# Tabled places for the side streams of an attention turn, and 22 idle products a turn, in a transformer block with routed experts

## The chip, the cores and the metric

The kernel runs on one core of one Trainium2 chip. The metric is the device time of one execution in microseconds. The core has five engines with one instruction row each, which wait for one another by semaphores: TensorE (PE; its weight loads are PEld), VectorE (DVE), ScalarE (ACT), GpSimd (POOL) and SyncE (SP), which here only issues DMAs.

## What is computed

Sixteen sequences of 512 tokens with 128 channels pass through one block: a modulated layer norm, causal attention with 16 heads of 8 channels and rotary positions, a gated residual; then a second norm and a feed-forward layer in which every token goes to 8 of 160 experts, beside one shared expert.

```python
mod = (silu(c) @ wmod)                         # sa, ca, ga, sb, cb, gb for each sequence
h = layernorm(x) * (1 + ca) + sa
q, k, v = split(h @ qkv_w.T + qkv_b)           # q and k rotated (apply_rope)
attn = softmax(where(causal, q @ k.T / sqrt(8), -1e9))
x = x + ga * ((attn @ v) @ proj_w.T + proj_b)
h = layernorm(x) * (1 + cb) + sb
top_w, top_idx = top_k(sigmoid(h @ router_w.T + bias), 8)
x = x + gb * (sum over the 8 experts of silu(h @ w_gate) * weight @ w_down + shared(h))
```

## The kernel before, in words

The program has two parts. The first goes through the attention and the routing of all sequences, in turns numbered -2 to 16; the second runs the experts over pages of 128 gathered tokens and adds up their results. The change touches only the first.

**The core of a turn.** Turn i does two things side by side. It finds the row maxima of the scores of sequence i+1, in 40 units of one bank each: TensorE multiplies q by k (L558, bf16, into banks 0 and 1, called MX), and VectorE takes the maximum (the custom instruction at L568, which writes rmax). And it computes the exponentials of sequence i (the first ten units still of sequence i-1), again 40 units: TensorE multiplies k by q with the maxima folded in (L645, into banks 2 to 4, called ST), adds the causal mask by small products (L657), and ScalarE takes the exponential (L672, which writes prob). The units go in pairs. A pair of maximum products comes first, then a pair of score products, 20 of each in a turn; I count them from 0. Between them stand the steps of `attend`: four groups of products of prob with v (L708, into bank 5), a copy by ScalarE (L717), four transposes (L722) and a normalisation by VectorE (L729, L734). A unit may write its bank only when the unit before it in that bank has been read: `begin` waits for VectorE's count s_mxd, or for ScalarE's count s_exa. At the turn's start the finished maxima are turned by three transposes (L596), the mark by which turns are cut below.

**The side streams.** Around this core each turn carries other work, each a list of steps:

- `pre(i + 2)`: 14 steps that prepare the sequence after next. First norm (L389 to L410, rstd on GpSimd L402), transposes (L423), then for q and for k a product (L441) that VectorE turns by the cosine (L447), a second product (L452) turned by the sine (L456), their sum (L463), a split into three bf16 parts by ScalarE and GpSimd, and a store by SP (L496); v (L507).
- `routing(i - 1)[:17]`: transposes of the attention's result (L836), the projection (L847), the gate on ScalarE (L851), transposes back (L858), the residual (L863), the second norm (statistics from L868, rstd2 on GpSimd L879, L886 for the norm), its transposes (L894), the router's products (L914, L915), and VectorE's search for the 8 best (L938, L982, L946, L953).
- `routing(i - 2)[17:]`: 14 steps that count tokens by expert and give each its place in a page (L989 to L1116, with the ranking products L1056 to L1059).
- scatters of tokens to pages by GpSimd (L783), loads of the score stacks, clears of pages.

**What sets the order.** `merge` lays all streams of a turn on a line from 0 to 1. A stream has a start and an end; step k of n is put at start + share x (k + 0.5), with share = (end - start) / n, and the parts of a step on different engines follow each other over `lag` x share. Everything is sorted by place, and each engine gets its parts in that order. So the places of the steps set each engine's row, and an engine does its row strictly in order. `pre` lies from 0.02 to 0.84, the first routing part from 0.53 to 0.98, the second from 0.0 to 0.46, all with even spaces and a lag of 0.6.

## Time and profile before

| | us |
|---|---|
| median of 3 runs | 2299.26 |
| lowest and highest | 2274.3, 2300.19 |
| the profiled execution, its own time | 2273.22 |
| its span, first to last instruction | 2271.2 |
| TensorE busy | 1653.4 (73%) |
| VectorE busy | 1261.6 (56%) |
| GpSimd busy | 1016.0 (45%) |
| ScalarE busy | 835.2 (37%) |
| mean granted TensorE clock | 0.819 |

Busy time is the union of an engine's instructions; register, branch and semaphore instructions and the issue of DMAs are not in it. Where an engine waits, the views name what ended the wait (releaser). Ends of matmuls are modelled. The granted clock is a share of 2.4 GHz; a fp32 matmul stands in the trace as two records. "x2" behind a row is the number of records merged into it, and its second number is the time from the start of the first to the end of the last.

### The profile page before, as it was taken

Reading aid. Unit: us, or ns where it says so; the run is one execution under the profiler, and the core shown is the slowest. Engines: PE = TensorE matmul, PEld = TensorE weight load, DVE = VectorE, ACT = ScalarE, POOL = GpSimd, SP = SyncE. Lnnn points to the kernel's source line nnn. Section 1 sums busy time; section 2 is a strip of 40 time slices with the busy share of each in tenths; the row PEclk is TensorE's granted clock in tenths of the full one; section 3 lists DMA queues with packets and bytes.
Section 4 is the critical chain, followed back from the end, with each engine's and each line's share of the span. In section 5 each row is a group of like instructions: output and inputs, shape, how many; then the busy total and the mean of one; then the engine's idle time right before and its main releaser. Section 6 shows DMA issues by size and latency. Waiting matters only on the chain. (4 is left out here: it accounts for less than half of the span.)

```text
span 2271.2 us, 33972 instructions
## 1 busy us (share of the span) xinstructions
PE 1653.4 (73%) x10822; PEld 766.5 (34%) x10822; DVE 1261.6 (56%) x4230; ACT 835.2 (37%) x1717; POOL 1016.0 (45%) x1054
## 2 busy tenths in 40 slices
PE   5667887887787887777776795466867777766774
PEld 2123333333333333333332563233433333333331
DVE  4757777776777777777753552023433334333347
ACT  1144444444444444444443432223323333322221
POOL 2000554565555555555553004444455555445552
PEclk9988887778877777788785897679889889888897
DMA  4875554455554445545332797646666666656431
GB/s 149 251 234 148 137 151 145 130 146 151 146 146 132 146 142 143 147 142 152 104 101 78 228 339 242 186 126 191 200 185 183 182 176 196 182 177 190 148 107 51
DMA packets 264985, 369.71 MB, mean 163 GB/s; under 512 B 41207, under 2 KB 141704, under 8 KB 264680
## 3 DMA queue, kind: packets, MB, share of 16 engines
q1 hardware_dynamic: 214248, 268.91, 40.9%
q0 software_dynamic: 28672, 58.78, 8.9%
q10 hardware_dynamic: 21888, 39.86, 4.7%
q8 instruction: 88, 1.44, 0.3%
q14 instruction: 89, 0.73, 0.1%
HBM read 219.79 MB, written 147.60 MB: 162 GB/s over the span
## 5 line engine op out<-in xcount | busy, mean ns | idle before, releaser
L1597 POOL DMA_INDIRECT vh<-results,pos_all x448 | 438.6, 979 | 547.4 <-DMA results<-v_ext 229.8
L783 POOL DMA_INDIRECT pages<-h,pos_s x448 | 439.0, 980 | 315.9 <-PE bank L558 123.0
L568 DVE CUSTOM_DVE_ANT_0 shelf<-bank,cb_all 128x512 bf16<-128x512 f32 (+3 forms) x1024 | 444.3, 484 | 187.5 <-PE bank L558 134.3
L672 ACT ACTIVATE prob<-bank 128x512 f32<-128x512 f32 x640 | 348.5, 595 | 408.4 <-PE bank L657 306.2
L1676 DVE TENSOR_TENSOR work<-work,bank 128x512 f32<-128x512 f32 x160 | 109.8, 686 | 494.8 <-ACT work L1670 253.6
L558 PE MATMUL bank<-km,qm 64*128 64x512 bf16 (+3 forms) x1024 | 213.5, 356 | 131.8 <-DVE rmax L568 91.2
L708 PE MATMUL bank<-prob,v_ext 128*32 128x512 f32 (+3 forms) x2048 | 247.4, 560 | 14.3 <-issue 12.4
L645 PE MATMUL bank<-qe,ke 64*128 64x512 bf16 (+3 forms) x1024 | 168.0, 344 | 62.7 <-ACT prob L672 36.2
L1560 ACT ACTIVATE v_ext<-bank 128x256 f32<-128x256 f32 x254 | 86.5, 383 | 289.4 <-remote 157.1
L1546 PE MATMUL bank<-prob,ke 64*128 64x128 f32 x1216 | 117.2, 315 | 88.1 <-ACT ke L1538 49.0
L1670 ACT ACTIVATE work<-bank 128x512 f32<-128x512 f32 x160 | 96.2, 601 | 190.7 <-PE bank L1658 99.3
L558 PEld LDWEIGHTS bank<-km,qm 64*128 64x128 bf16 x1024 | 51.5, 98 | 298.7 <-issue 146.2
L1546 PEld LDWEIGHTS bank<-prob,ke 64*128 64x128 f32 x1216 | 87.3, 202 | 183.2 <-issue 117.8
L1658 PE MATMUL bank<-vh,on_att 128*128 128x512 f32 x160 | 95.5, 682 | 62.1 <-ACT work L1670 36.6
L1530 PE MATMUL bank<-qe,prob 128*64 128x128 f32 x1216 | 108.1, 302 | 44.7 <-issue 33.6
L645 PEld LDWEIGHTS bank<-qe,ke 64*128 64x128 bf16 x1024 | 50.4, 97 | 195.7 <-issue 138.6
L1509 PE MATMUL bank<-c_all,prob 128*128 128x128 f32 x608 | 108.1, 303 | 5.5 <-issue 3.5
L657 PE MATMUL bank<-cb_all 64*128 64x128 bf16 (+1 forms) x1280 | 108.9, 227 | 0.0
L1611 DVE TENSOR_REDUCE oT<-vh 128x128 f32<-128x1024 f32 x56 | 106.6, 1903 | 1.9
L1538 ACT ACTIVATE ke<-bank 128x256 f32<-128x256 f32 x152 | 58.8, 387 | 107.7 <-remote 66.2
L475 POOL TENSOR_TENSOR work<-work,shelf 128x512 f32<-128x512 f32 x32 | 37.1, 1159 | 135.2 <-ACT shelf L469 134.8
L1520 ACT ACTIVATE qe<-bank 128x512 f32<-128x512 f32 x102 | 61.4, 602 | 84.4 <-remote 64.4
(209 smaller groups left out, 2469.1 us busy)
## 6 DMA issues: line engine op xcount, KB each, us to landing
prob<-wexp SPq DMA_DIRECT2D x448, 96.0 KB
pages<-free_rows SPq DMA_DIRECT2D x38, 1024.0 KB
prob<-pages SPq DMA_DIRECT2D x152, 256.0 KB
results<-v_ext ACTq DMA_DIRECT2D x152, 256.0 KB
qm<-q_stacks SPq DMA_DIRECT2D x64, 256.0 KB
km<-k_stacks SPq DMA_DIRECT2D x64, 256.0 KB
qe<-q_stacks SPq DMA_DIRECT2D x64, 256.0 KB
ke<-k_stacks SPq DMA_DIRECT2D x64, 256.0 KB
```

The costliest lines, as they stand in the source:

```text
L558: last = e.matmul(MX[g % 2][:, c0:c0 + (i + 1) * P], qm[rows_, c % 2, h, i * P:(i + 1) * P], km[rows_, c % 2, h, 0:(i + 1) * P], start=Tru ...
L568: last = e.tensor_tensor_reduce(out=masked[:, g % 2, c0:c0 + (i + 1) * P], in0=MX[g % 2][:, c0:c0 + (i + 1) * P], in1=mask_w[:, S - (i + 1 ...
L645: e.matmul(ST[g % 3][:, c0:c0 + S - j * P], ke[rows_, c % 2, h, j * P:(j + 1) * P], qe[rows_, c % 2, h, j * P:S], start=(k == 0), stop=Tru ...
L657: return e.matmul(out_, pick[rows_, :], over, start=False, stop=True, skip_group_check=True)
L672: e.activation(prob[:, slot, :], ST[g % 3][:, :], ACT.Exp, scale=SCALE).then_inc(s_exa, 1)
L708: last = e.matmul(PV[32 * g:32 * g + 32, j * P:S], v_ext[:, j, 4 * c + g, :], prob[:, (c % 2) * UNITS + u, c0:c0 + S - j * P], start=(j == ...
L783: e.indirect_dma_start(out=pages, in_=h2[:, t, :], in_offset=None, out_offset=bass.IndirectOffsetOnAxis(ap=pos_s[:, t * TOPK + k:t * TOPK ...
L1509: last = e.transpose(TX[G % 2][:, :].rearrange("d (p q) -> d q p", q=GRP)[:, q, :], x_in[G % DEEP][:, q, :], ident)
L1530: last = e.matmul(GT[half:half + 64, (j // 2) * P:(j // 2 + 1) * P], w_gate(G, j), x_T[G % 2][:, j * P:(j + 1) * P], start=True, stop=True)
L1546: last = e.matmul(YP[j % 2][:, (j // 2) * D:(j // 2 + 1) * D], h_g[G % 2][half:half + 64, (j // 2) * P:(j // 2 + 1) * P], w_down(G, j), st ...
L1597: e.indirect_dma_start(out=y8[:, i, k, :], out_offset=None, in_=results[0:ready(n) * GRP * P, :], in_offset=bass.IndirectOffsetOnAxis(ap=p ...
L1676: e.tensor_tensor(f_hw[u % 2], f_h[u % 2], FC[:, :], ALU.mult).then_inc(s_dm, 1)
```

## The change

It has two parts.

1. `merge` takes tables in place of a start and an end. `pre` for turns 0 to 13 (PRE_AT, PRE_LATE), the first routing part for turns 1 to 14 (FIRST_AT, FIRST_LATE) and the second for turns 2 to 15 (SECOND_AT, SECOND_LATE) get one place a step, and one lateness a step in place of `lag`. Each stream keeps its own order; what moves is how the streams lie to one another and to the core.
2. `exp_unit` returns a fifth function, `idle`: a product of the identity with the first 128 to 512 columns of the cosine table (fp32), written to the bank that this score unit writes next, whose result is overwritten by it. It waits for the count of ScalarE that the score unit waits for. `pair` calls it ahead of a pair. The table IDLE has 20 numbers for the maximum pairs and 20 for the score pairs, in columns; 11 of each are above zero. This holds in the turns 1 to 14. The bank of an idle product ahead of a maximum pair is that of the next score pair.

```diff
--- before.py
+++ after.py
@@ -86,11 +86,14 @@
 
     timed = []
     for order, (steps, start, end, *lag) in enumerate(streams):
-        share = (end - start) / len(steps)
         for k, step in enumerate(steps):
+            if isinstance(start, tuple):
+                at, late = start[k], end[k]
+            else:
+                share = (end - start) / len(steps)
+                at, late = start + share * (k + 0.5), share * (lag[0] if lag else 0.9)
             for j, (name, f) in enumerate(step.items()):
-                at = start + share * (k + 0.5 + j * (lag[0] if lag else 0.9) / max(len(step) - 1, 1))
-                timed.append((at, order, k, j, {name: f}))
+                timed.append((at + j * late / max(len(step) - 1, 1), order, k, j, {name: f}))
     return [t[-1] for t in sorted(timed, key=lambda t: t[:4])]
 
 
@@ -670,16 +673,23 @@
                     wait(e, s_pv, 4 * n + c - 1)
                 slot = (c % 2) * UNITS + exp_place(pieces[0][0], par, pieces[0][1])[0]
                 e.activation(prob[:, slot, :], ST[g % 3][:, :], ACT.Exp, scale=SCALE).then_inc(s_exa, 1)
-            return begin, step, len(pieces) + 2, expo
-
-        def pair(*units):
+            def idle(e, cols):
+
+                if cols:
+                    wait(e, s_exa, n * 4 * UNITS + g - prev + 1)
+                    e.matmul(ST[g % 3][:, 0:cols], ident, cosT[:, 0:cols], start=True, stop=True)
+            return begin, step, len(pieces) + 2, expo, idle
+
+        def pair(*units, idle=None):
 
             def pe(e):
-                for begin, product, _, _ in units:
+                if idle is not None:
+                    idle(e)
+                for begin, product, *_ in units:
                     begin(e)
                     product(e, 0)
                 for k in range(1, 4):
-                    for _, product, n, _ in units:
+                    for _, product, n, *_ in units:
                         if k < n:
                             product(e, k)
             return pe
@@ -760,7 +770,10 @@
                 behind = behind[0] if behind else []
                 if gm:
                     units = [max_unit(nm, g) for g in gm]
-                    steps.append({"pe": pair(*units), "dve": lambda e, us=units: [u[3](e) for u in us]})
+                    idle = None
+                    if ge and nm > 1:
+                        idle = lambda e, f=exp_unit(ge[0][0] // 4, ge[0][0] % 4 * UNITS + ge[0][1])[4], cols=IDLE[gm[0] // 2]: f(e, cols)
+                    steps.append({"pe": pair(*units, idle=idle), "dve": lambda e, us=units: [u[3](e) for u in us]})
                     for g in gm:
                         if g in (UNITS + 1, 2 * UNITS + 1):
                             steps.extend(max_loads(nm, [g // UNITS + 1]))
@@ -769,7 +782,10 @@
                 steps += behind[0:1]
                 if ge:
                     units = [exp_unit(q // 4, q % 4 * UNITS + u) for q, u in ge]
-                    steps.append({"pe": pair(*units), "act": lambda e, us=units: [u[3](e) for u in us]})
+                    idle = None
+                    if gm and nm > 1:
+                        idle = lambda e, f=units[0][4], cols=IDLE[2 * UNITS + gm[0] // 2]: f(e, cols)
+                    steps.append({"pe": pair(*units, idle=idle), "act": lambda e, us=units: [u[3](e) for u in us]})
                 steps += behind[1:2]
             if i == NB:
                 steps += attend(4 * NB - 1)
@@ -1316,6 +1332,16 @@
 
 
         HALF, SHARE, AHEAD1 = 17, 18, 8
+        PRE_AT = (0.014, 0.093, 0.104, 0.204, 0.283, 0.41, 0.483, 0.483, 0.529, 0.581, 0.634, 0.674, 0.706, 0.722)
+        PRE_LATE = (0.049, 0.037, 0.001, 0.039, 0.032, 0.006, 0.015, 0.021, 0.008, 0.051, 0.052, 0.007, 0.035, 0.052)
+        FIRST_AT = (0.546, 0.613, 0.645, 0.682, 0.769, 0.769, 0.794, 0.811, 0.847, 0.864, 0.897, 0.904, 0.904, 0.904,
+                    0.917, 0.934, 0.951)
+        FIRST_LATE = (0.01, 0.019, 0.022, 0.016, 0.034, 0.01, 0.006, 0.002, 0.001, 0.012, 0.001, 0.011, 0.005, 0.031,
+                      0.035, 0.016, 0.01)
+        SECOND_AT = (0.0, 0.024, 0.104, 0.113, 0.139, 0.139, 0.192, 0.249, 0.255, 0.282, 0.341, 0.425, 0.449, 0.499)
+        SECOND_LATE = (0.011, 0.013, 0.023, 0.031, 0.031, 0.04, 0.01, 0.036, 0.026, 0.02, 0.032, 0.019, 0.009, 0.017)
+        IDLE = (512, 0, 0, 384, 128, 0, 128, 0, 256, 128, 128, 0, 0, 256, 256, 384, 0, 0, 128, 0, 0, 128, 256, 256,
+                512, 128, 0, 0, 128, 384, 0, 0, 256, 256, 384, 0, 0, 0, 0, 256)
 
         def turn_a(i):
 
@@ -1346,15 +1372,19 @@
                 streams.append((max_loads(1, (0,)), 0.86, 0.86))
                 streams.append((max_loads(1, (1,)), 0.98, 0.98))
             elif i < NB - 2:
-                streams.append((pre(i + 2), 0.02, 0.84, 0.6))
+                streams.append((pre(i + 2), PRE_AT, PRE_LATE))
                 streams.append((max_loads(i + 2, (0, 1)), 0.87, 0.92))
             if i == NB - 1:
                 streams.append(([gate_step(q) for q in range(4)], 0.05, 0.6))
                 streams.append((table(), 0.55, 0.9))
                 streams.append(([{"sp": picks_in}], 0.1, 0.1))
-            if 2 <= i <= NB:
+            if 2 <= i < PAGED + 2:
+                streams.append((routing(i - 2)[HALF:], SECOND_AT, SECOND_LATE))
+            elif i == NB:
                 streams.append((routing(i - 2)[HALF:], 0.0, 0.46, 0.6))
-            if 1 <= i < NB:
+            if 1 <= i <= PAGED:
+                streams.append((routing(i - 1)[:HALF], FIRST_AT, FIRST_LATE))
+            elif i == NB - 1:
                 streams.append((routing(i - 1)[:HALF], 0.53, 0.98, 0.6))
             if 3 <= i < NB:
                 streams.append(paced(scatters(i - 3)[SHARE:], i, 0.0, 0.4))
```

In the new program that makes 308 more products: 112 of 128 columns, 112 of 256, 56 of 384 and 28 of 512. Line numbers from L97 up to the idle products shift by three, those behind by 10 to 30: L558 is now L561, L568 L571, L645 L648, L672 L675, L708 L718, L722 L732, L452 L455, L858 L874, L894 L910. The idle products are L680.

How TensorE's row changes is shown at three places of one turn, first before, then after (rows of the same unit forms merged).

Around the third and fourth pair of a turn (L645 and L657 are score products, L558 maximum products, L1035 spreads the page table, L423 transposes the first norm), before:

```order
L645 MATMUL bank<-qe,ke 128x512 x2
L657 MATMUL bank<-cb_all 128x64 x4
L558 MATMUL bank<-km,qm 128x384 x2
L558 MATMUL bank<-km,qm 128x128 x2
L1035 MATMUL bank<-rows,ones_row 128x320
L423 MATMUL bank<-c_all,work 128x128 x4
L645 MATMUL bank<-qe,ke 128x384 x2
```

and after (L648, L660, L561, L1051):

```order
L680 MATMUL bank<-c_all 128x256
L648 MATMUL bank<-qe,ke 128x512 x2
L660 MATMUL bank<-cb_all 128x64 x4
L1051 MATMUL bank<-rows,ones_row 128x320
L680 MATMUL bank<-c_all 128x384
L561 MATMUL bank<-km,qm 128x384 x2
L561 MATMUL bank<-km,qm 128x128 x2
L680 MATMUL bank<-c_all 128x256
L648 MATMUL bank<-qe,ke 128x384 x2
L648 MATMUL bank<-qe,ke 128x128 x2
L660 MATMUL bank<-cb_all 128x2x64 x4
```

The transposes of the first norm are gone from here (they stand two groups earlier), and idle products of 256, 384 and 256 columns stand ahead of three pairs.

Around the sixth and seventh pair, where the second rotated product of q (L452) stands, before:

```order
L657 MATMUL bank<-cb_all 128x2x64 x4
L558 MATMUL bank<-km,qm 128x512 x2
L645 MATMUL bank<-qe,ke 128x512 x2
L657 MATMUL bank<-cb_all 128x64 x4
L452 MATMUL bank<-work,w_all 128x512
L708 MATMUL bank<-prob,v_ext 32x512 x4
L558 MATMUL bank<-km,qm 128x384 x2
L558 MATMUL bank<-km,qm 128x128 x2
L1056 MATMUL bank<-filled,cb_all 128x160
```

and after (L455; L1072 to L1075 are the ranking products):

```order
L680 MATMUL bank<-c_all 128x128
L648 MATMUL bank<-qe,ke 128x512 x2
L660 MATMUL bank<-cb_all 128x64 x4
L1072 MATMUL bank<-filled,cb_all 128x160
L1074 MATMUL bank<-chosen,cb_all 128x160 x2
L1075 MATMUL bank<-chosen,cb_all 128x160
L1072 MATMUL bank<-filled,cb_all 128x160
L1074 MATMUL bank<-chosen,cb_all 128x160 x3
L1075 MATMUL bank<-chosen,cb_all 128x160
L455 MATMUL bank<-work,w_all 128x512
L718 MATMUL bank<-prob,v_ext 32x512 x4
L680 MATMUL bank<-c_all 128x128
```

The rotated product now comes behind the seven ranking products, which stood behind the next maximum pair, and no longer right behind the score pair.

Where the second norm is transposed (L894; L507 is v, L722 transposes the attention's result, L914 and L915 are the router's), before:

```order
L657 MATMUL bank<-cb_all 128x2x64 x4
L507 MATMUL bank<-w_all,work 128x128 x4
L722 MATMUL bank<-c_all,oT 128x128 x4
L558 MATMUL bank<-km,qm 128x256 x4
L645 MATMUL bank<-qe,ke 128x256 x4
L657 MATMUL bank<-cb_all 128x2x64 x4
L894 MATMUL bank<-c_all,xn 128x128 x4
L558 MATMUL bank<-km,qm 128x512 x2
L914 MATMUL bank<-eb_part,cb_all 128x160
```

and after (L910):

```order
L648 MATMUL bank<-qe,ke 128x256 x4
L660 MATMUL bank<-cb_all 128x2x64 x4
L680 MATMUL bank<-c_all 128x384
L561 MATMUL bank<-km,qm 128x512 x2
L648 MATMUL bank<-qe,ke 128x512 x2
L660 MATMUL bank<-cb_all 128x64 x4
L718 MATMUL bank<-prob,v_ext 32x512 x4
L561 MATMUL bank<-km,qm 128x384 x2
L561 MATMUL bank<-km,qm 128x128 x2
L718 MATMUL bank<-prob,v_ext 32x384 x4
L910 MATMUL bank<-c_all,xn 128x128 x4
```

Between the transposes of the attention's result and those of the norm there are now two more pairs and two groups of products with v (L718), with two idle products of 384 columns.

## Rows read from the trace of the kernel before

**Rows 1.** The page of the kernel before: span, busy time, clock by slices.

```profile
span 2271.2 us, 33972 instructions
...
PE 1653.4 (73%) x10822; PEld 766.5 (34%) x10822; DVE 1261.6 (56%) x4230; ACT 835.2 (37%) x1717; POOL 1016.0 (45%) x1054
...
PEclk9988887778877777788785897679889889888897
```

**Rows 2.** Busy time by turn (start:end, length, busy us, clock, DMA share, GB/s).

```profile
568.60:642.80 74.20, 59.27 (x426) 24.36 (x426) 54.05 (x233) 33.00 (x64) 40.32 (x43) 0.78 0.50 142
...
790.00:868.20 78.20, 62.30 (x425) 24.96 (x425) 54.42 (x233) 33.94 (x66) 40.15 (x43) 0.72 0.47 138
...
1014.60:1087.40 72.80, 55.65 (x426) 23.24 (x426) 54.01 (x233) 32.84 (x64) 40.40 (x43) 0.80 0.51 147
sum 882.50, PE 700.14 PEld 288.22 DVE 649.72 ACT 394.68 POOL 470.83; mean PE 58.35 PEld 24.02 DVE 54.14 ACT 32.89 POOL 39.24
```

**Rows 3.** The same view, cut where the clock changes in one turn; and one later stretch.

```profile
572.60:579.40 6.80, 4.42 (x50) 1.63 (x46) 6.56 (x27) 2.19 (x5) 4.96 (x5) 1.00 0.61 184
579.40:593.00 13.60, 12.16 (x55) 4.48 (x53) 8.85 (x35) 5.11 (x10) 4.94 (x6) 0.50 0.48 137
...
620.40:634.00 13.60, 12.61 (x62) 4.83 (x62) 6.12 (x29) 4.79 (x10) 9.34 (x10) 0.50 0.56 136
1300.00:1400.00 100.00, 86.49 (x916) 61.17 (x914) 49.87 (x99) 38.14 (x91) 8.97 (x10) 0.98 0.96 319
```

**Rows 4.** TensorE's row in time, one turn: waits in brackets, with their releaser.

```profile
578.09 0.33 PE L558 MATMUL bank<-km,qm 64*128 64x384 bf16 x1 [1.93 <-issue]
...
588.60 0.61 PE L645 MATMUL bank<-qe,ke 64*128 64x512 bf16 x2 [0.83 <-ACT prob L672]
...
589.92 2.08 PE L452 MATMUL bank<-work,w_all 128*128 128x512 f32 x2 [0.60 <-DVE work L447]
...
599.02 0.33 PE L558 MATMUL bank<-km,qm 64*128 64x384 bf16 x2 [0.28 <-DVE rmax L568]
...
603.69 0.39 PE L645 MATMUL bank<-qe,ke 64*128 64x256 bf16 x3 [2.07 <-ACT prob L672]
...
605.19 0.39 PE L558 MATMUL bank<-km,qm 64*128 64x512 bf16 x1 [0.23 <-DVE rmax L568]
...
612.43 0.66 PE L858 MATMUL bank<-c_all,on_att 128*128 128x128 f32 x4 [1.10 <-ACT on_att L851]
...
617.78 0.28 PE L558 MATMUL bank<-km,qm 64*128 64x256 bf16 x1 [0.45 <-DVE rmax L568]
618.47 0.39 PE L558 MATMUL bank<-km,qm 64*128 64x256 bf16 x3 [0.41 <-DVE rmax L568]
...
621.04 1.11 PE L894 MATMUL bank<-c_all,xn 128*128 128x128 f32 x4 [1.85 <-DVE xn L886]
...
641.22 1.21 PE L558 MATMUL bank<-km,qm 64*128 64x512 bf16 x2 [1.73 <-DVE rmax L568]
```

**Rows 5.** VectorE in the same turn, in time, around TensorE's waits at 578.1 and 621.0.

```profile
574.70 0.53 DVE L1004 TENSOR_TENSOR_SCAN endp<-newp,endp,zero_row 1x160 f32<-1x160 f32 x1
...
577.35 0.67 DVE L568 CUSTOM_DVE_ANT_0 shelf<-bank,cb_all 128x512 bf16<-128x512 f32 x1
...
618.34 2.65 DVE L886 TENSOR_SCALAR xn<-xr,mv,rstd 128x128 f32<-128x128 f32 x4
```

**Rows 6.** The same row in time: one fp32 product of 512 columns at full clock.

```profile
600.16 1.02 PE L441 MATMUL bank<-work,w_all 128*128 128x512 f32 x2
```

**Rows 7.** Who waited for whom in that turn (us in total, times, longest).

```profile
ACT prob L672 <- PE bank L657: 20.3, 11, 5.7
...
DVE shelf L568 <- PE bank L558: 9.9, 4, 6.9
...
PE bank L558 <- DVE rmax L568: 4.2, 9, 1.7
```

**Rows 8.** The page's group of exponentials (count, busy us, mean ns, idle before).

```profile
L672 ACT ACTIVATE prob<-bank 128x512 f32<-128x512 f32 x640 | 348.5, 595 | 408.4 <-PE bank L657 306.2
```

## Prediction

> **What bounds the kernel now.** I read the page first: TensorE is the busiest engine (73% of the span), VectorE is next (56%), and the granted TensorE clock goes up and down all through the first half [rows 1]. The change acts only inside the attention turns, so the next view is busy time cut at one mark that comes once a turn (the transposes of L596). Twelve full turns, from 204.9 to 1087.4 us, take 882.5 us, 73.5 each; of that TensorE is busy 58.35, VectorE 54.14, GpSimd 39.24 and ScalarE 32.89 [rows 2]. No engine is full: TensorE stands idle some 15 us in each. And its clock is 0.72 to 0.80 in the turns shown. The clock has two levels, 2.4 and 1.2 GHz, so a mean of 0.78 says that TensorE spent 44% of the turn at the lower one. The turns also rank by it: 78.20 us at 0.72, 74.20 at 0.78, 72.80 at 0.80.
>
> I take the turn from 568.6 to 642.8 as the pattern (74.2 us, 59.27 busy, clock 0.78). Cut where its clock changes, it reads [rows 3]: a stretch at full clock with TensorE busy 4.42 of 6.8 us, then 13.6 us at half clock in which it is busy 12.16; later again 13.6 at half, busy 12.61. So the clock falls after a piece with long waits, and at half clock TensorE is nearly always busy, because it is then the slow one. Its waits in that turn are few and long [rows 4]: 1.93 us ahead of a pair of maximum products at 578.1, 2.07 ahead of score products at 603.7, 1.85 ahead of the transposes L894 at 621.0, 1.73 at 641.2, 1.10 ahead of L858, and 0.83 + 0.60 around L452. They add up to 10.1 of the 14.9 us idle. Behind the 1.93 stands VectorE, which in those microseconds does eight steps of the side streams in its order, from 574.7 to 577.4, before the two reductions that would free the banks [rows 5]. So what bounds a turn is a chain that goes back and forth between TensorE and VectorE, stretched wherever side steps are bunched, and stretched again by the half clock that follows.
>
> A model of the turn for the sums below: at half clock TensorE was busy 0.91 of the time (24.77 of 27.2 us), so of 32.6 us at half clock 14.8 us are what the lower clock costs. The work at full clock is 59.3 - 14.8 = 44.5, idle 14.9, together 59.4, and turn = 59.4 / (1 - 0.455 x L), with L the share of time at half clock; with L = 0.44 it gives 74.3.
>
> **The change part by part.**
>
> *The products added.* Each turn gets 22, with 5,632 columns, as much as 11 products of 512 columns. They are fp32, 128 rows, 128 columns of weights, as L441 is. One L441 of 512 columns is two records and takes 1.02 us at full clock [rows 6]; L452, of the same form, takes 2.08 at half [rows 4]. So a turn gets 11 x 1.02 = 11.2 us of TensorE at full clock (22.9 if all at half). What of it lies in waits, where a product counts as covered as far as its pair waited at its first or its second unit [rows 4]: 512 columns ahead of the pair that waited 1.73 (covers 1.02), 384 ahead of 1.93 (0.77), 256 ahead of 0.45 + 0.41 (0.51), 384 ahead of the score pair that waited 2.07 (0.77), 128 ahead of 0.83 (0.26), 128 ahead of 0.23 (0.23), and three ahead of waits of 0.28 like the one at 599.0 (0.27 each). Together 4.4. The other 6.8 us stand where the trace shows no wait, and lengthen TensorE's row by that.
> The profile's rows put a price of 1.02 us on 512 fp32 columns. The Trainium skill, page "Perfetto Trace Analysis", section "Engine Utilization", puts fp32 at half of the full output rate; by that, 512 columns would be 0.43 us and the added work 4.7 us a turn. The row disagrees by more than two, and the measurement decides.
>
> *The wait added.* Each idle product waits until ScalarE has read the bank that the next score pair writes. Ahead of a maximum pair this is new: behind it stand the maximum products, and behind those VectorE. ScalarE, though, is busy 33 of 74 us and itself waits 20.3 us in that turn for TensorE's last score products [rows 7], so the bank is mostly free long before. I take 0; at worst each of the 11 ahead of maximum pairs waits for one exponential of 0.595 us [rows 8], 6.5 us a turn. Nothing below zero is possible here, as no wait is taken away.
>
> *The places moved.* No work is added or removed; three chains change their distance. The rotated projection (L452, now L455) moves from right behind the score pair to behind the ranking products, so VectorE's L447 is done in time: 0.83 + 0.60 us. The transposes of the second norm (L894, now L910) come after two more groups of products, while the norm on VectorE (2.65 us for four [rows 5]) stays near its place: 1.85. The gate's transposes (L858, now L874) come a group later than the projection they wait for: 1.10. That is 4.4 us at most. But the same steps land elsewhere in VectorE's one line, where reductions wait behind them: in the new order paging and the first norm are still bunched at the place of the 1.93. I take 2.0 us recovered; bounds 4.4 and -1.5 (a new bunch that costs what the smaller of the old ones does). On GpSimd the step rstd moves past a few scatters; GpSimd is busy 39 of 73.5 us (40.32 for 43 instructions in the turn, 0.94 each [rows 2]) and the norm behind it was moved later too, so 0, at worst one scatter a turn, 1 us. On SP the key store goes from 0.81 to 0.72 of the turn, ahead of the last load of the score stacks; if its data is late, that load waits, but it is wanted only in the next turn, over 16 us on: 0.
>
> *The clock.* With the above, the work at full clock is 44.5 + 11.2 = 55.7 and idle 14.9 - 4.4 - 2.0 = 8.5, together 64.2. TensorE would be busy 0.87 of the time at full clock, against 44.5 of 59.4 = 0.75 now. In the stretch from 1300 to 1400 us it is busy 0.865 of the time, and the granted clock is 0.98 there [rows 3]. That is the upper end; 0.78, as now, is the lower. In a turn the waits come bunched, so I take a value between, a little above the middle because 512 and 384 columns stand exactly in the waits at which the clock fell: 0.90, L = 0.20.
>
> *The sum.* 64.2 / (1 - 0.455 x 0.20) = 70.6 us a turn, 3.6 less than 74.2. There are 14 turns with added products and about as many with new places: 50 us. The profiled execution took 2273.2 us (its span 2271.2), so 2223. Its time is 26 us under the median of the three runs, 2299.3, and one of the three was as fast (2274.3). The same ratio on the median gives 2248. I put the forecast between, at 2235.
>
> **The rivals.**
>
> *The clock doesn't answer, and the products are bare cost.* Place: the 6.8 us of products that stand in no wait. For it: no wait of TensorE in the turn is over 2.07 us, and still the clock fell, so what remains of them can go on pulling it down, and at half clock each added product costs double. Against: the falls come with the bunched waits, where the longest products stand. With 0.80, L = 0.40: 64.2 / 0.818 = 78.5, 4.3 more a turn, 60 in all: 2333 against the profiled time, 2345 between it and the same ratio on the median. It decides below a clock of 0.85, where the formula gives 74.2 again. With the tables bringing nothing either it is 66.2 / 0.818 = 80.9 a turn, 94 us more.
> The skill's page "TensorE: Matmul & The Clock Gate", section "Why this matters for your kernels", warns only of long idle gaps between bursts; by it this kernel's clock should never fall and filling short gaps would bring nothing, which is this rival. That the clock fell in a turn with no wait over 2.07 us [rows 3, 4] speaks against the rule.
>
> *VectorE holds the turn.* It is busy 54 of 73.5 us in one fixed order, and 9.9 of its idle microseconds in that turn are waits for TensorE's maximum products [rows 7]. If the clock rises, TensorE arrives earlier and waits longer for reductions; the idle products only fill that. Then a turn loses perhaps 0 to 1.5 us: 2273 - 10 = 2263, and 2275 between profile and median. For it: TensorE's maximum products already wait 4.2 us in that turn for reductions, nine times [rows 7]. Against: VectorE waits more than twice as long for them, 6.9 us at once.
>
> *The clock goes up whole.* With 0.98, as in 1300 to 1400: 64.2 / 0.982 = 65.4, 8.8 less a turn, 123 in all: 2150.
>
> **How the numbers follow.** Forecast 0.42, VectorE holds 0.28, clock doesn't answer 0.16, clock whole 0.14. The time is the forecast's, 2235. About 2% (46 us) is what a measurement of this kernel tells from no change: faster means under 2253. The forecast's own spread (clock 0.87 to 0.93) is 72.8 to 68.6 us a turn, about 2265 to 2205, so most of it is faster; with the whole clock and a little of the VectorE case that is 0.50. Slower (over 2345) is about half of the bare-cost case and what the added wait could do at worst: 0.14. The rest, 0.36, is within 2%. The range leaves out the upper part of the bare-cost case and the end of the whole-clock case: 2165 to 2330.
>
> **What would show it right or wrong.** Right: the granted clock of the full turns at 0.87 to 0.93; TensorE busy about 60 us a turn in spite of the added 11; turns of 69 to 72 us; the waits ahead of L910, L455 and L874 gone; ahead of the 512- and 384-column products a shorter wait. Wrong: a clock under 0.85; VectorE idle under 12 us a turn, with TensorE waiting for its reductions as long as now; or idle products that wait for ScalarE. The parts outside the turns should not move by over 5 us.

## The result, and the profile after

The changed kernel takes 2261.99 us (median of 20 runs, 2247.07 to 2274.14), the kernel before 2279.07 (median of 20, 2255.83 to 2309.58); the ratio is 0.9949, with a 95% interval of 0.9924 to 0.9974. That is less than the 2% which the prediction calls faster, but the interval lies below 1, so it is a gain; 2235 had been forecast. In this measurement and in the two sets e11 to e14 and e15 to e18 the kernel before takes 2258 to 2279 us, in all other sets 1936 to 1941, and one chip showed both (1941 in the set e1 to e4, 2258 in e11 to e14), so every ratio here is taken inside its own set, and the two conditions are called "at 2270" and "at 1940".

The page of the changed kernel, to be held against [rows 1]: TensorE is busy 64 us more, the slices of the clock in the first half read 8 and 9 where they read 7 and 8. The group below them is the added products (two records each).

```profile
span 2248.9 us, 35204 instructions
...
PE 1717.5 (76%) x11438; PEld 830.0 (37%) x11438; DVE 1267.9 (56%) x4230; ACT 828.5 (37%) x1717; POOL 1007.9 (45%) x1054
...
PEclk9979898889988899889886997788887889888987
...
L680 PE MATMUL bank<-c_all 128*128 128x128 f32 (+3 forms) x616 | 229.0, 456 | 7.9 <-ACT prob L675 7.9
```

Where the 22 us between the two profiled executions went is read from windows cut at the same mark as [rows 2] (start:end, length, busy us of PE, PEld, DVE, ACT, POOL, clock, DMA share, GB/s): turn 0, turn 1, the twelve full turns, turn 14, the rest. First the kernel before, in the pieces that were not shown ahead:

```profile
84.60:147.40 62.80, 38.50 (x267) 15.27 (x267) 35.57 (x155) 21.57 (x41) 5.63 (x5) 0.85 0.88 274
147.40:204.90 57.50, 47.64 (x403) 20.12 (x401) 43.25 (x194) 31.66 (x61) 7.00 (x6) 0.89 0.52 147
204.90:1087.40 882.50, 700.14 (x5101) 288.22 (x5101) 649.72 (x2785) 394.68 (x768) 470.83 (x493) 0.78 0.50 143
1087.40:1148.90 61.50, 50.52 (x404) 21.32 (x405) 46.05 (x214) 27.96 (x56) 34.09 (x37) 0.78 0.34 90
1148.90:2271.20 1122.30, 768.83 (x4531) 405.34 (x4531) 439.71 (x693) 350.29 (x777) 485.01 (x498) 0.83 0.58 175
```

The same pieces of the changed kernel:

```profile
85.45:152.14 66.69, 41.85 (x270) 15.12 (x270) 37.34 (x164) 21.38 (x41) 6.64 (x6) 0.86 0.86 257
152.14:212.10 59.96, 56.72 (x451) 25.22 (x449) 42.72 (x187) 31.89 (x62) 5.61 (x5) 0.93 0.50 142
212.10:1067.89 855.79, 746.09 (x5631) 343.30 (x5629) 654.74 (x2787) 388.62 (x768) 462.99 (x492) 0.89 0.52 148
1067.89:1135.74 67.85, 56.87 (x447) 26.26 (x445) 45.73 (x211) 29.45 (x59) 33.65 (x37) 0.87 0.29 79
1135.74:2248.90 1113.16, 768.25 (x4527) 403.88 (x4527) 440.00 (x692) 348.12 (x773) 485.54 (x498) 0.84 0.58 176
```

A full turn goes from 73.5 to 71.3 us (26.7 us in all). Its clock rises from 0.78 to 0.89, TensorE is busy 62.2 instead of 58.3, idle 9.1 instead of 15.2. Turns 0, 1 and 14 get longer, by 3.9, 2.5 and 6.4, which takes back half. The rest, where only the second routing table in turn 15 was changed, is 9.1 shorter; in the profiles of e11 to e18 it ranges from 1093 to 1130 us, so that is inside what it varies by.

TensorE's waits over the twelve full turns (us in total, times, longest), first of the kernel before:

```profile
PE bank L558 <- DVE rmax L568: 59.8, 119, 2.8
...
PE bank L894 <- DVE xn L886: 22.2, 12, 1.9
...
PE bank L858 <- ACT on_att L851: 7.2, 6, 1.2
PE bank L452 <- DVE work L447: 6.6, 8, 2.1
```

and of the changed one:

```profile
PE bank L930 <- issue: 32.9, 13, 5.1
PE bank L561 <- DVE rmax L571: 13.8, 41, 0.9
PE bank L910 <- DVE xn L902: 11.1, 11, 1.1
PE bank L648 <- ACT prob L675: 8.9, 13, 1.0
...
PE bank L680 <- ACT prob L675: 7.2, 12, 0.7
...
PE bank L874 <- ACT on_att L867: 3.1, 2, 2.3
```

Waits for reductions come to 1.2 us a turn, where the kernel before has 5.0; the transposes of the second norm wait 0.9 instead of 1.85; those of the gate, with a row named "issue" of 2.3 us beside the one shown, 0.45 instead of 0.6; the rotated projection is in no row at all. An idle product itself waits for ScalarE 0.6 us once a turn. The largest row stands in a new place: 2.7 us a turn ahead of the router's products L930, put down to nothing ("issue"). Rows of that name together are as long in both kernels, 3.9 us a turn (47.3 and 46.5 us in twelve), and nearly absent from their traces at 1940 (0.2 and 4.3 us).

What that wait is can be read from the instructions around it. In turn 4 of the changed kernel, and ScalarE's waits at L939 over the twelve turns:

```profile
411.05 0.54 PE L931 MATMUL bank<-w_all,h2T 128*128 128x160 f32 x2
...
411.52 0.64 PE L718 MATMUL bank<-prob,v_ext 128*32 128x256 f32 x8
...
414.02 0.44 ACT L939 ACTIVATE logit<-bank 128x320 f32<-128x320 f32 x1 [2.86 <-remote]
...
414.52 0.31 PE L930 MATMUL bank<-eb_part,cb_all 3*128 3x160 bf16 x1 [2.36 <-issue]
```

```profile
ACT logit L939 <- remote: 57.9, 15, 5.7
```

The router's products come in two groups, and the second (its first product is L930) may write only when ScalarE has read the result of the first (L939); L939 waits for the last product of the first group (L931). That one ends at 411.59 in the trace; L939 starts 2.4 us later, L930 right after L939 has ended. In eleven of the twelve turns it is so: L939 starts 1.8 to 5.2 us after the end of its product, where 0.04 us is usual, and L930 starts 0.05 to 0.06 us after L939 has ended. So the new order does not make this wait by itself (e5, the same kernel at 1940, has no such row); a TensorE product was reported done late. The experiments e15 to e18 come back to it.

### The profile page after: what moved, and what is told of

Same layout as the page of the kernel before. It is cut to its first block and busy times, and to the rows that moved or that the text cites. A ratio compares the mean times of both kernels' runs of the same rounds, so it can differ in the third digit from the quotient of the medians.

```text
span 2248.9 us, 35204 instructions
## 1 busy us (share of the span) xinstructions
PE 1717.5 (76%) x11438; PEld 830.0 (37%) x11438; DVE 1267.9 (56%) x4230; ACT 828.5 (37%) x1717; POOL 1007.9 (45%) x1054
## 5 line engine op out<-in xcount | busy, mean ns | idle before, releaser
L571 DVE CUSTOM_DVE_ANT_0 shelf<-bank,cb_all 128x512 bf16<-128x512 f32 (+3 forms) x1024 | 445.4, 485 | 144.8 <-PE bank L561 110.5
L675 ACT ACTIVATE prob<-bank 128x512 f32<-128x512 f32 x640 | 348.3, 597 | 410.5 <-PE bank L660 329.9
L680 PE MATMUL bank<-c_all 128*128 128x128 f32 (+3 forms) x616 | 229.0, 456 | 7.9 <-ACT prob L675 7.9
L561 PE MATMUL bank<-km,qm 64*128 64x512 bf16 (+3 forms) x1024 | 171.0, 333 | 55.3 <-DVE rmax L571 35.5
L718 PE MATMUL bank<-prob,v_ext 128*32 128x512 f32 (+3 forms) x2048 | 203.7, 475 | 11.7 <-issue 9.7
L648 PE MATMUL bank<-qe,ke 64*128 64x512 bf16 (+3 forms) x1024 | 151.0, 331 | 33.3 <-ACT prob L675 21.2
L680 PEld LDWEIGHTS bank<-c_all 128*128 128x128 f32 x616 | 102.5, 205 | 90.6 <-issue 70.0
L561 PEld LDWEIGHTS bank<-km,qm 64*128 64x128 bf16 x1024 | 43.7, 96 | 199.4 <-DVE rmax L571 98.9
L1568 ACT ACTIVATE ke<-bank 128x256 f32<-128x256 f32 x152 | 58.8, 387 | 111.1 <-remote 86.2
L660 PE MATMUL bank<-cb_all 64*128 64x128 bf16 (+1 forms) x1280 | 96.9, 221 | 0.0
```

The costliest lines, as they stand in the source:

```text
L561: last = e.matmul(MX[g % 2][:, c0:c0 + (i + 1) * P], qm[rows_, c % 2, h, i * P:(i + 1) * P], km[rows_, c % 2, h, 0:(i + 1) * P], start=Tru ...
L571: last = e.tensor_tensor_reduce(out=masked[:, g % 2, c0:c0 + (i + 1) * P], in0=MX[g % 2][:, c0:c0 + (i + 1) * P], in1=mask_w[:, S - (i + 1 ...
L648: e.matmul(ST[g % 3][:, c0:c0 + S - j * P], ke[rows_, c % 2, h, j * P:(j + 1) * P], qe[rows_, c % 2, h, j * P:S], start=(k == 0), stop=Tru ...
L675: e.activation(prob[:, slot, :], ST[g % 3][:, :], ACT.Exp, scale=SCALE).then_inc(s_exa, 1)
L680: e.matmul(ST[g % 3][:, 0:cols], ident, cosT[:, 0:cols], start=True, stop=True)
L718: last = e.matmul(PV[32 * g:32 * g + 32, j * P:S], v_ext[:, j, 4 * c + g, :], prob[:, (c % 2) * UNITS + u, c0:c0 + S - j * P], start=(j == ...
```

## The experiments

All figures in one table. "Turn" is the mean of the twelve full turns of the profiled run, then its clock, TensorE's busy and idle time in it, and the length of turn 14. (The kernel before, first measurement: 73.5, 0.78, 58.3, 15.2, 61.5; the changed one 71.3, 0.89, 62.2, 9.1, 67.9.)

| run | what it is | before | ratio, 95% | turn | clock | busy | idle | turn 14 |
|---|---|---|---|---|---|---|---|---|
| e6 | the kernel before | 1936 | 1.001 (0.997 to 1.005) | 70.9 | 0.79 | 57.9 | 13.0 | 57.7 |
| e1 | tables alone | 1941 | 0.940 (0.938 to 0.943) | 61.6 | 0.87 | 50.9 | 10.7 | 59.9 |
| e2 | products alone | 1941 | 0.983 (0.980 to 0.986) | 67.7 | 0.94 | 61.0 | 6.7 | 56.3 |
| e3 | tables and waits | 1941 | 0.942 (0.939 to 0.944) | 61.3 | 0.88 | 51.1 | 10.2 | 59.9 |
| e4 | trimmed | 1941 | 0.956 (0.953 to 0.958) | 63.9 | 0.96 | 58.5 | 5.4 | 58.1 |
| e5 | the changed kernel | 1936 | 0.959 (0.956 to 0.963) | 63.9 | 0.96 | 58.4 | 5.6 | 56.1 |
| e7 | 16-bit products | 1938 | 0.939 (0.936 to 0.942) | 60.1 | 0.92 | 51.8 | 8.3 | 57.1 |
| e8 | tables, turn 0 even | 1938 | 0.942 (0.939 to 0.945) | 61.2 | 0.88 | 50.8 | 10.4 | 56.8 |
| e9 | first-norm table alone | 1938 | 0.992 (0.989 to 0.995) | 68.9 | 0.82 | 55.6 | 13.3 | 61.0 |
| e10 | tables alone | 1938 | 0.941 (0.938 to 0.944) | 61.3 | 0.88 | 51.0 | 10.2 | 56.8 |
| e11 | before, delays | 2258 | 1.034 (1.027 to 1.040) | 77.9 | 0.76 | 60.1 | 17.8 | 66.6 |
| e12 | changed, delays | 2258 | 1.020 (1.015 to 1.026) | 74.9 | 0.90 | 62.9 | 12.0 | 68.9 |
| e13 | tables alone, delays | 2258 | 1.014 (1.010 to 1.018) | 74.0 | 0.78 | 57.9 | 16.2 | 71.0 |
| e14 | first routing table alone | 2258 | 0.988 (0.985 to 0.992) | 71.0 | 0.81 | 54.7 | 16.2 | 62.4 |
| e15 | tables alone | 2264 | 0.988 (0.983 to 0.993) | 70.7 | 0.79 | 56.7 | 14.0 | 69.7 |
| e16 | products alone | 2264 | 0.999 (0.995 to 1.002) | 72.4 | 0.90 | 63.9 | 8.6 | 59.6 |
| e17 | the changed kernel | 2264 | 0.993 (0.989 to 0.996) | 71.0 | 0.91 | 61.7 | 9.3 | 67.7 |
| e18 | 16-bit products | 2264 | 0.988 (0.983 to 0.993) | 71.6 | 0.79 | 60.1 | 11.5 | 69.4 |

### One part alone (e1, e2, e3)

Tables alone set the numbers of IDLE to nought (no product, no wait):

```diff
-        IDLE = (512, 0, 0, 384, 128, 0, 128, 0, 256, 128, 128, 0, 0, 256, 256, 384, 0, 0, 128, 0, 0, 128, 256, 256,
...
+        IDLE = (0,) * (4 * UNITS)
```

Products alone put the even places back (here one of three streams):

```diff
-                streams.append((pre(i + 2), PRE_AT, PRE_LATE))
+                streams.append((pre(i + 2), 0.02, 0.84, 0.6))
```

The third keeps the added waits and leaves out the products, which are no part of what is computed:

```diff
                     wait(e, s_exa, n * 4 * UNITS + g - prev + 1)
-                    e.matmul(ST[g % 3][:, 0:cols], ident, cosT[:, 0:cols], start=True, stop=True)
```

Expected, tables alone:

> The tables of places alone, no idle product. Theory A (products buy clock with work, tables remove waits): the full turn keeps a clock near 0.79, waits fall from 15 to about 12 us, the turn of 73.5 us becomes 71.5 to 73; time 0.98 to 1.0 of before. Rival B (the clock doesn't matter, the tables are the whole gain): the same turn as with both, 71.3 us or less, ratio 0.985 to 0.995. Rival C (tables were fitted to the products and lose without them): a ratio over 1.0.

Expected, products alone:

> The 22 idle products alone, with the old even places. Theory A: the clock of the full turns rises from 0.78 to about 0.88, TensorE is busy 62 to 64 us a turn, and the turn stays within 1 us of 73.5, ratio 0.995 to 1.01. Rival B (bare cost): clock rises but no turn gets shorter, each uncovered product adds its time, 6.8 us a turn at most, ratio 1.02 to 1.04.

Expected, tables and waits:

> The changed kernel whose idle products are left out while the waits for ScalarE ahead of the pairs are kept: it tells what the added wait costs. If the wait costs nothing (my prediction took 0), it equals the kernel with tables alone within 0.3%. If it costs, it is slower than that by up to 0.6 us in the turn for the one place where TensorE waits for ScalarE at L680 (x14 turns = 8 us, 0.4%), more if other places join.

Measured: 1826.43, 1906.85 and 1828.98 us, against 1940.78. The tables are worth 6.0%, the products 1.7%, the added waits nothing that can be told (e3 lies 0.14% over e1, each known to about 0.25%). The ranges expected of e1 and e2 all missed: they had been set for a kernel before of 2279 us, and the gains are larger than any of them allowed. The surprise is in the clock of the tables alone, 0.87 in the full turns where the kernel before has 0.79: the new order, with 10.7 us idle instead of 13.0, lifts it with no product added.

### The changed kernel, trimmed, and both kernels again (e4, e5, e6)

e4 leaves the products out of turns 1 and 14 (one of the two places of the edit is shown) and keeps the even places of the first norm in turn 0:

```diff
-                    if ge and nm > 1:
+                    if ge and 2 < nm < 15:
```

> The changed kernel without idle products in turns 1 and 14, and with the old even places of the preparing stream in turn 0. Against the kernel before, turn 0 went from 62.8 to 66.7 us, turn 1 from 57.5 to 60.0, turn 14 from 61.5 to 67.9: 12.8 us together. Theory A (there the products are bare cost, since less other work lies beside the core, and the table of the preparing stream is no good for a turn without routing): those three turns fall back to 181.8 us in all, ratio 0.989. Rival: the turns 0, 1 and 14 vary by themselves from run to run, and the ratio stays 0.995.

> The changed kernel, unaltered, beside the kernel before. In the first four experiments the kernel before took 1941 us instead of 2279, and its waits woke up at once, where in the trace of the prediction one in ten took half a microsecond more. Theory D (two conditions of the machine, in which waits cost differently): under the quick condition the changed kernel takes 0.955 to 0.965 of before, as its trimmed version did (0.956), and its idle products are bare cost against the tables alone (0.940). Rival: the quick condition changes nothing in the comparison, and the ratio is 0.995 again; then the trim of turns 0, 1 and 14 brought 4%.

> The kernel before, unaltered, for its trace under the same condition as the other experiments. Theory D: full turns of 65 to 67 us instead of 73.5, VectorE busy 54 as before, TensorE's idle time 8 to 11 us instead of 15, and a wait of ScalarE for TensorE ends 50 ns after its release in nine of ten cases. Rival: its turns are 73 us and the difference lies in the experts' part alone.

Measured: 1855.5, 1860.57 and 1942.03 us. At 1940 the changed kernel is 4.1% faster than the one before; on top of the tables its products cost 2% (34 us). The trims bring back turns 0 and 1 (63.4 and 56.7 us against 66.2 and 59.9 in e5), lose 2.0 in turn 14, and leave the full turns alone: 0.3% between two sets, inside their intervals.

e5 is what its first theory expected. e6 is not: its turns of 70.9 us with 13.0 idle stand against 65 to 67 with 8 to 11. The windows of its full turns and of all behind turn 14:

```profile
204.06:1054.69 850.63, 694.38 (x5101) 284.36 (x5101) 648.06 (x2785) 393.98 (x768) 470.56 (x493) 0.79 0.53 149
1112.41:1944.50 832.09, 697.25 (x4531) 380.90 (x4531) 440.19 (x693) 354.24 (x774) 509.98 (x498) 0.92 0.75 236
```

Of the 327 us between the two traces of the kernel before, 32 lie in the twelve full turns and 290 behind turn 14, where the experts are computed and next to nothing of this change acts (1122.3 and 832.1 us; the DMA engines move 175 and 236 GB/s there). That is nearly the rival of e6.

### 16-bit products, turn 0, one table, and the tables again (e7 to e10)

e7 makes the same products of 16-bit operands (its edit is shown); e8 is the tables alone with turn 0 as in e4; e9 keeps of the tables only PRE, without products.

```diff
-                    e.matmul(ST[g % 3][:, 0:cols], ident, cosT[:, 0:cols], start=True, stop=True)
+                    e.matmul(ST[g % 3][:, 0:cols], identb, cb_all[:, 0:cols], start=True, stop=True)
```

> The changed kernel, with the 22 idle products made of 16-bit operands (the 16-bit unit matrix and 16-bit constants) in the same places, of the same columns, with the same waits. The score products of 512 columns have 16-bit operands too and cost about a quarter of the 1.02 us that 512 fp32 columns take, so the added work should fall from 11.2 to about 2.8 us a turn at full clock. Theory 'the clock answers to the time that TensorE is busy': little cover is left, the granted clock falls back near the 0.899 of the tables alone (0.90 to 0.91), and the time is that of the tables alone within 1%: ratio 0.935 to 0.950. Rival 'a product there is what counts, however short': the clock stays near the 0.944 of the changed kernel while the work is 8 us a turn less: ratio 0.91 to 0.93.

> The tables alone (no idle products, no added waits), but in the first turn the first norm and projection keep their even places, as before. Turn 0 took 62 to 63 us with even places and 65 to 66 with the table, in both pairs of kernels. Theory 'the table was made for full turns and fits turn 0 badly': turn 0 comes back to 62 to 63 us, the rest stays, the kernel is 3 us (0.2%) faster than the tables alone. Rival 'turn 0 is longer because more of turn 1 is drawn into it': turn 1 is longer by as much, and nothing is won.

> Of the tables only the one for the next block's norm and projections (14 steps) is in place; both parts of the routing keep their even places; no idle products. The tables together brought 6.0% where they ran alone (about 116 us, some 8 a turn). The prediction's terms were the rotated projection behind the ranking products (0.83 + 0.60 us, this table) and the transposes of the second norm and the gate (1.85 + 1.10 us, the routing tables). Theory 'each table mends its own chain': this one brings a third, ratio 0.975 to 0.985. Rival 'the gain is in the three together, in VectorE's one order, where every bunch stands in front of reductions': below a fifth of it alone, ratio 0.988 to 1.00. If this table carries nearly all, the ratio is 0.94 to 0.96.

> The tables alone once more, beside the others of this set. Where the kernel before takes about 1940 us, the ratio should be 0.940 again, within 0.004. Where it takes about 2280 us, with the late starts that its trace showed, the two theories part: if the idle products are what brought little there too, the tables alone are 0.96 to 0.98; if the late starts eat the tables' gain, they are 0.99 to 1.00, as the changed kernel was.

Measured: 1818.57, 1824.15, 1921.41 and 1823.88 us against 1938.20. With cheap products the 2% are gone: the price was TensorE's own time. Their clock, 0.92 in the full turns, lies between the tables' 0.88 and the fp32 products' 0.96, so it answered in part, and what it gave paid for them and no more. (The trace of e7 lacks 28 of the 308 products, so its busy time is a little too low.) e8: turn 0 is back at 62.5 us (65.4 in e10), turn 1 as long as there (56.0, 55.9), but the 3 us are under what the times can tell. e9: this table brings 2.0 us a turn, 0.8% of the 6.0%, as its rival expected ("the gain is in the three together"); whether the routing's tables bring the rest by themselves, no run at 1940 tells.

### Delays put in, and the first routing table (e11 to e14)

The traces of both kernels at 2270 have instructions that start half a microsecond and more after what they waited for had ended; those at 1940 have next to none. e11 to e13 put delays into the three kernels: every seventh exponential, and the first piece of every seventh reduction, is done twice, the second time after the first has ended, with the same result (the edit of the exponential is shown). e14 keeps of the tables only FIRST, without products or delays.

```diff
+                if g % 7 == 0:
+                    e.activation(prob[:, slot, :], ST[g % 3][:, :], ACT.Exp, scale=SCALE).then_inc(s_twice_a, 1)
+                    e.wait_ge(s_twice_a, n * 6 + g // 7 + 1)
                 e.activation(prob[:, slot, :], ST[g % 3][:, :], ACT.Exp, scale=SCALE).then_inc(s_exa, 1)
```

> The kernel before, with every seventh exponential and the first piece of every seventh maximum reduction done twice, the second after the first has ended (6 of each in a sequence, the same result): 6 x 0.6 us on ScalarE and 6 x 0.48 us and more on VectorE in each turn, in front of what waits for them. It stands for the late starts of about 0.5 us and more that the traces of the kernel before and of the changed one showed where they took 2273 and 2251 us (58 exponentials and 21 reductions in twelve turns of the changed one). Theory 'late starts cost what the turn has no waits for': this kernel has 12.7 to 13.6 us of waits of TensorE in a turn and loses little, 1 to 3 us a turn, ratio 1.005 to 1.02. Rival 'a delay costs its own length in any of the kernels': about 6.5 us a turn, ratio 1.04 to 1.05.

> The changed kernel with the same delays as in the kernel before of this set. Without them it was 0.959 of the kernel before, with 5 to 6 us of waits of TensorE in a turn. Theory 'late starts cost what the turn has no waits for': it loses more than the kernel before does, 4 to 7 us a turn, ratio 0.985 to 1.01, so that what it gains on the kernel before shrinks to 0 to 2%, as in the measurement at 2279 us. Rival 'a delay costs the same in any of the kernels': the distance to the kernel before with delays stays at 4%.

> The tables alone with the same delays. Without them 0.9405, with 9 to 10 us of waits of TensorE in a turn. Theory 'late starts cost what the turn has no waits for': between the two others, 2 to 5 us a turn, ratio 0.955 to 0.98; then the products are what makes the changed kernel tender. If it loses as much as the changed kernel (over 5 us a turn, ratio over 0.98), the tighter order is what makes both tender, and the products have no part in it. If all three lose alike, delays of this kind don't explain the small gain.

> Of the tables only the one for the first 17 steps of the routing (second half of a turn: the output projection, the second norm, the transposes L910) is in place, no idle products. The table for norm and projections alone brought 0.8% of the 6.0%. The prediction put the 1.85 us ahead of the transposes of the second norm and the place of VectorE's bunch behind this part. Theory 'the second norm's bunch is the main one': ratio 0.955 to 0.975. If it brings less than 1.5%, the gain lies in the second part of the routing, or only in all three together.

Measured: 2340.45, 2313.75, 2287.7 and 2238.31 us against 2257.99. The machine was at 2270, so the delays came on top of its own. The ranges expected of them, set for 1940, can't be held against them. With e15 and e17 of another set as the undelayed ones, the kernel before loses 3.4%, the changed one 2.8% (1.020 less 0.993), the tables alone 2.6%, each known to about 0.7%. The three can't be told apart, and the kernel with the longest waits did not lose less: the theory that late starts are harmless where a turn has waits gets no support, for delays of this kind, and what e13 called "all three lose alike" is what stands. The first routing table alone brings 1.2%, less than the 2.5 to 4.5% expected of it at 1940, and as much as the three tables together at 2270 (e15).

### The change taken apart at 2270 (e15 to e18)

> The tables alone, where the kernel before takes about 2260 us. With the delays put in, the tables alone were 0.977 of the kernel before with the same delays (2287.7 to 2340.5 us) and the changed kernel 0.989. Theory 'the tables gain about 2% here, and the products take back over 1%': ratio 0.970 to 0.985, below the changed kernel of this set by 0.010 to 0.020. Rival 'the late starts eat the tables' gain': 0.99 to 1.00, and no better than the changed kernel. If the kernel before takes about 1940 us, 0.940 again.

> The idle products (22 a turn, fp32, and their waits) with the old even places. 0.983 where the kernel before takes 1940 us. Theory 'the products take back what the clock gives, once late starts leave fewer of them in a wait': 1.00 to 1.015 here. Rival 'they gain here as there': 0.98 to 0.99.

> The changed kernel once more: 0.995 as at first, within 0.005, if the kernel before takes about 2260 to 2280 us; 0.959 if it takes 1940.

> The changed kernel with idle products of 16-bit operands, a quarter of the time each. At 1940 us it was 0.939, level with the tables alone, the clock 0.02 higher. Theory 'the price of the fp32 products is their own time on TensorE': here too it is level with the tables alone within 0.005, or up to 0.01 better. Rival 'it is the waits and the place in the order that cost, not the time of the product': as the changed kernel of this set, about 0.995.

Measured: 2240.81, 2260.03, 2245.86 and 2232.16 us against 2263.60. Here too the tables are what gains (1.2%), the fp32 products bring nothing that can be told (0.1%, the interval holds 1), and with both it is 0.7%, in agreement with the 0.5% of the first measurement. The distance between the tables alone and both, 0.5%, is inside the intervals; its sign is that of the 2% at 1940. Held against what was expected, e15 falls between its theory (0.970 to 0.985) and its rival, e16 lies at the lower end of its theory (1.00 to 1.015), e17 and e18 came as expected. The 16-bit products, level with the tables alone in time, leave the clock of the full turns at the tables' 0.79 here. The windows of full turns, turn 14 behind the first and the second; tables alone, products alone, both, 16-bit products:

```profile
206.95:1055.55 848.60, 680.66 (x5101) 290.31 (x5101) 648.99 (x2785) 388.24 (x768) 464.32 (x493) 0.79 0.53 149
1055.55:1125.28 69.73, 52.74 (x404) 22.39 (x404) 46.52 (x214) 29.62 (x59) 33.45 (x37) 0.72 0.28 78
```

```profile
210.04:1078.86 868.82, 766.26 (x5631) 346.15 (x5629) 647.17 (x2785) 395.47 (x768) 468.09 (x492) 0.90 0.51 146
1078.86:1138.44 59.58, 54.64 (x448) 24.97 (x446) 45.91 (x213) 28.38 (x56) 33.78 (x37) 0.93 0.35 95
```

```profile
211.70:1063.50 851.80, 740.19 (x5631) 340.39 (x5629) 654.87 (x2786) 388.65 (x768) 463.28 (x492) 0.91 0.52 149
```

```profile
205.27:1064.99 859.72, 721.19 (x5364) 302.29 (x5364) 650.08 (x2785) 387.76 (x768) 465.61 (x493) 0.79 0.52 147
```

And the tables alone at 1940 (e10), for the first of them:

```profile
205.92:941.06 735.14, 612.44 (x5101) 267.18 (x5101) 635.17 (x2788) 386.82 (x768) 463.95 (x492) 0.88 0.61 172
```

The same program, the same counts of products, 9.5 us a turn apart, and the clock at 0.79 instead of 0.88. Where the time sits is in VectorE's waits over the full turns, e15 first, then e10:

```profile
DVE shelf L571 <- remote: 73.3, 12, 6.7
DVE shelf L571 <- PE bank L561: 38.4, 29, 2.5
DVE v L954 <- ACT logit L939: 31.8, 12, 7.1
DVE xr L879 <- remote: 30.8, 10, 3.1
```

```profile
DVE shelf L571 <- PE bank L561: 49.0, 44, 2.1
DVE v L954 <- ACT logit L939: 28.1, 10, 2.8
```

"Remote" is a semaphore count for which the trace has no instruction that ended within the 1.5 us before it. It is the same reduction once in each turn. In time, e15, turn 3:

```profile
328.22 0.39 PE L561 MATMUL bank<-km,qm 64*128 64x512 bf16 x2
...
330.56 0.64 PE L718 MATMUL bank<-prob,v_ext 128*32 128x256 f32 x8
...
334.24 0.69 DVE L571 CUSTOM_DVE_ANT_0 shelf<-bank,cb_all 128x512 bf16<-128x512 f32 x1 [6.66 <-remote]
334.35 0.44 ACT L939 ACTIVATE logit<-bank 128x320 f32<-128x320 f32 x1 [2.39 <-remote]
334.51 0.95 POOL L799 DMA_INDIRECT pages<-h,pos_s  x1 [1.66 <-remote]
334.84 0.31 PE L930 MATMUL bank<-eb_part,cb_all 3*128 3x160 bf16 x1 [3.64 <-issue]
```

And the same place in e10:

```profile
316.67 0.39 PE L561 MATMUL bank<-km,qm 64*128 64x512 bf16 x2
...
317.09 0.69 DVE L571 CUSTOM_DVE_ANT_0 shelf<-bank,cb_all 128x512 bf16<-128x512 f32 x1 [0.93 <-PE bank L561]
...
318.76 0.64 PE L718 MATMUL bank<-prob,v_ext 128*32 128x256 f32 x8
...
319.36 0.24 PE L930 MATMUL bank<-eb_part,cb_all 3*128 3x160 bf16 x1
```

In e10 the reduction starts as soon as its product ends and TensorE goes on without a pause. In e15 it starts 5.6 us after its product ended (328.61), and four engines start again within 0.6 us. The semaphore events kept in the trace say what each of them waited for. The count of the L561 products, for which VectorE and GpSimd wait, came at 334.21 and 334.25; that of the router's products, which ended at 330.63, at 334.32, and ScalarE waits for it; TensorE's L930 waits for that ScalarE instruction, which ended at 334.78. So all four go back to TensorE's own products. Their ends in the trace are modelled: whether the products were late or only their counts, it doesn't tell.

It is so everywhere. In each of the ten traces at 2270 (before, changed, e11 to e18), 274 to 326 waits were ended by a count that came over 0.4 us after the end of its instruction, and that instruction was a TensorE product every time; in the ten traces at 1940 there is not one. "Remote" rows, too, stand in all of the former and in none of the latter. In e15 VectorE has such a row once in every turn at L571 and in ten of the twelve turns at L879; in other kernels they stand at other places. So the delays at 2270 are of another kind than those put in: longer, and they come from TensorE's products, not from ScalarE's and VectorE's instructions.

## Why the prediction was right or wrong

**The products added: right.** Put the measured turns into the prediction's own model, S = turn x (1 - 0.455 x L), where S is work at full clock and idle time together (a hundredth of clock is 0.6 to 0.7 us of S, so differences of 1 us are at its edge; at 2270 the kernel before has its trace from the first measurement, the parts from e15 to e18). Before: 73.5 and L = 0.44 give 58.8. Products alone (e16): 72.4 and 0.20 give 65.8, that is 7.0 more; at 1940, 67.7 at 0.94 against 70.9 at 0.79 give 64.0 and 57.3, 6.7 more. 6.8 bare microseconds had been forecast, from 1.02 us for 512 fp32 columns. The Trainium skill, page "Perfetto Trace Analysis", section "Engine Utilization", halves TensorE's output rate for what it calls FP32_LOW_HIGH. By that price, an estimate, the added work is 4.7 us, and S could not rise by more even with none of it covered; the 7.0 do not bear it out. The 16-bit products add about 1 us to S (60.1 at 0.92 against 61.3 at 0.88 at 1940, 55.7 and 54.6).

**The wait added: right at 1940.** Taken at 0; e3 lies 0.14% over e1, inside what the times can tell. It is not tested alone at 2270; in the changed kernel's trace an idle product waits 0.6 us for ScalarE once a turn.

**The places moved: right in size for the work, short in what they do.** S falls by 1.6 at 2270 (e15: 70.7 at L = 0.42 gives 57.2) and by 2.7 at 1940 (61.3 at 0.24 gives 54.6), against 2.0. What the step left out is that the order can lift the clock by itself: 0.79 to 0.88 at 1940, and 0.78 to 0.79 at 2270, where 14.0 us of a turn stay idle. Of its single terms, 1.85 became 0.9, the waits at L452 (0.8 a turn on the mean) went, and the gate's 1.10, taken from one turn, is 0.6 before and 0.45 after. At 1940 the new S at the old clock would be a turn of 67.5 us (54.6 at L = 0.42), so 3.4 of the 9.6 us that a turn gains from the tables are places and 6.2 are clock. The prediction gave the clock to the products alone.

**The clock: right, 0.89 for 0.90.** S came out at 64.2, as predicted, in part by luck: it began 0.6 lower than forecast (58.8 for 59.4), and the products added 0.2 more and the places brought 0.4 less. But the clock's gain is what the products pay with: by the same model, the products alone buy 8.8 us a turn (58.8 at L = 0.44 and at 0.20) and cost 7.7 (7.0 at 0.20), at 1940 10.3 for 7.1. Two large terms that nearly cancel. With the tables in place the clock at 1940 is 0.88 already; the products then buy 4.6 (54.6 at 0.24 and at 0.08) for 7.3, and the turn gets 2.6 longer, as e10 and e5 show.

**The sum: the step that failed.** "There are 14 turns with added products and about as many with new places: 50 us" measured 14 us over all turns. It took one turn's forecast for all of them. Of the 28 us between 2223 and the profiled 2251, the full turns are 16.5: 43.2 forecast, 26.7 measured. Half of that is the pattern turn, 74.2 us against a mean of 73.5, the other half is 0.01 of clock. The shoulder turns are 19.9: 7.2 saved were forecast for turns 1 and 14 and nothing for turn 0, and the three grew by 12.7. Turn 0 is the first-norm table (e8 undoes it: 62.5 for 65.4 us); turn 1 the products (58.6 in e2 and 59.9 in e5 with them, 55.9 in e1 without; e4 undoes it); turn 14 the tables, but only at 2270 (69.7 with them, 59.6 with products alone, 57 to 60 with the tables alone at 1940), where the first routing table alone has 62.4. The rest, 8.3 the other way, lies outside the turns, inside what that part varies by. The base hid a little of the error: the forecast was put between the profiled time and a median of three runs, 2299, which over 20 runs is 2279. The same 50 us off 2279 would have been 2229, so the high median moved the forecast 6 us towards the measured time, by luck.

**The signs.** Most of those named for "right" came: clock 0.89, TensorE busy 62.2 us, turns of 71.3 us, no wait at L455, half of the one at L910. The wait at L874 stayed, an idle product waits for ScalarE, and the part outside the turns moved by 9 us. All but the last are signs of a full turn, and none of them tests the turns 0, 1 and 14, which is where most of the forecast was lost.

**The rivals.** "The clock doesn't answer" is wrong. "VectorE holds the turn" had the nearest time, 2263 to 2275, and not the mechanism: VectorE is idle 16.8 us a turn and TensorE waits 1.2 us for reductions. "The clock goes up whole" came at 1940 only (0.96).

**What stays open.** Why TensorE's products are reported done late at 2270, and why the tables gain 6% in one condition and 1.2% in the other, is not shown. What is shown: the late counts stand in all traces at 2270 and in none at 1940, and e15 has the lower clock with them. That they cause the small gain is argued from this alone. The kernel before loses 2.6 us a turn to that condition, products alone 4.7, both 7.1 to 7.4, the tables alone 9.5, the 16-bit products 11.5. The shorter a turn is at 1940, the more it loses; e11 to e13 speak against a plain lack of waits to hide a delay in, though for delays of another kind and put in at 2270 only. No run took the late counts away.

**The best version.** Not the changed kernel. The tables alone, with no product: 0.940 at 1940 and 0.988 at 2270; the 16-bit products are level with them (0.939, 0.988).

## What to carry to other kernels

A product that only keeps TensorE's clock up is paid in TensorE's own time, here 7 to 8 us a turn against 9 to 10 us of clock; use the cheapest operand type, and only where a wait is left after the order has been mended. Mend the order first and read the clock again: at 1940 the new order gave by itself 0.09 of clock, where the products gave 0.15; at 2270 it gave 0.01, and the time still fell by 1.2%. Work out a sum over all turns from the mean of all of them, and the first and last turns by themselves, since a table made for the full turn can lengthen those.
